# Five engines' written orders of one step, replaced by other orders of the same calls

## The reference

```
q, k, v = split(einsum(x, w_qkv) + b_qkv)        # q, k rotated
weights = softmax(mask(q k / sqrt(192) + alibi))
h = h + einsum(weights v, w_out) + b_out
```

## Time and profile before

| | |
|---|---|
| median of 3 runs | 1754.96 us (1750.04 to 1756.24) |
| the profiled execution | 1752.32 us, of which the span of the instructions is 1750.5 us |
| busy, of the span | TensorE 95%, VectorE 84%, ScalarE 76%, GpSimd 64% |
| mean granted TensorE clock | 0.976 of full |
| transfers | 113.70 MB, on average 65 GB/s |
| chain that ended last | 88% TensorE, 4% VectorE, 3% SyncE's queue, 2% GpSimd |

### The profile page before, as it was taken

The page is one execution under the profiler, slowest core; times in us unless marked ns, Lnnn a source line. Parts: engine busy times, 40 slices in busy tenths (PEclk is TensorE's granted clock), DMA queues, the critical chain, the costliest instruction groups (busy, mean ns, idle before and its releaser), DMA issues.

```text
span 1750.5 us, 48653 instructions
## 1 busy us (share of the span) xinstructions
PE 1664.2 (95%) x16742; PEld 1278.3 (73%) x16742; DVE 1470.0 (84%) x4972; ACT 1323.6 (76%) x3812; POOL 1120.1 (64%) x1034
## 2 busy tenths in 40 slices
PE   7758999999999999999999999999999999999975
PEld 6635777777777777777777777777777777777653
DVE  3837888899888888899888888899888888889874
ACT  0326888888888888888888888888888888888762
POOL 0087667766777666766777667666677667666500
PEclk9789999999999999999999999999999999999986
DMA  9311111111111111111111111111111111111100
GB/s 320 110 61 61 56 53 56 53 67 57 61 68 68 59 61 57 50 65 62 56 68 68 66 55 60 54 56 66 55 64 68 68 53 61 56 53 62 44 7 13
DMA packets 90168, 113.70 MB, mean 65 GB/s; under 512 B 14818, under 2 KB 52163, under 8 KB 89667
## 3 DMA queue, kind: packets, MB, share of 16 engines
q1 hardware_dynamic: 89922, 110.59, 18.1%
HBM read 26.62 MB, written 8.42 MB: 20 GB/s over the span
## 4 chain that ended last, share of the span: by engine, by line
PE 88%; DVE 4%; SPq 3%; POOL 2%; ACT 1%; issue 1%; DMA 0%; DVEq 0%; POOLq 0%; ACTq 0%
PE bank L725 45%; PE bank L842 9%; PE bank L983 7%; PE bank L831 6%; PE bank L829 6%; PE bank L994 3%; PE bank L853 3%; PE bank L903 3%; PE bank L891 2%; PE bank L1003 2%; SPq L320 1%; PE bank L882 1%; DVE arena L1283 1%; PE bank L950 0%; POOL rot L486 0%
## 5 line engine op out<-in xcount | busy, mean ns | idle before, releaser
L482 POOL TENSOR_TENSOR arena<-rq,cos 128x512 f32<-128x512 f32 x256 | 326.1, 1274 | 280.0 <-ACT rq L526 280.0
L535 ACT ACTIVATE arena<-arena,nm 128x129 f32<-128x129 f32 (+1 forms) x1024 | 455.6, 455 | 0.0
L486 POOL TENSOR_TENSOR rot<-rot,sin 128x512 f32<-128x512 f32 x256 | 326.3, 1275 | 103.9 <-DMA rot<-rq 103.9
L725 PE MATMUL bank<-xt_h,weights 128*128 128x256 f16 x2048 | 378.9, 273 | 9.2 <-ACT rq L526 7.8
L526 ACT ACTIVATE rq<-bank,bqk 128x256 f32<-128x256 f32 x512 | 214.4, 471 | 170.1 <-PE bank L725 155.3
L1283 DVE CUSTOM_DVE_ANT_0 arena<-bank,bias 128x129 f32<-128x129 f32 (+1 forms) x1024 | 317.9, 352 | 26.5 <-issue 16.6
L489 POOL TENSOR_TENSOR arena<-arena,rot 128x512 f32<-128x512 f32 x256 | 314.2, 1228 | 37.3 <-POOL rot L486 0.9
L1291 DVE TENSOR_TENSOR ptr_l<-bank,ptr_h 128x384 f16<-128x384 f32 x512 | 280.0, 552 | 31.8 <-ACT ptr_h L545 29.4
L545 ACT ACTIVATE ptr_h<-bank 128x384 f16<-128x384 f32 x512 | 249.1, 486 | 68.6 <-PE bank L725 44.0
L725 PE MATMUL bank<-xt_l,weights 128*128 128x256 f16 x1024 | 279.6, 273 | 0.0
L842 PE MATMUL bank<-eye,arena 128*128 128x128 f32 x1536 | 253.0, 277 | 8.5 <-DVE ptr_l L1291 4.4
(11 more groups left out here) (200 smaller groups left out, 3182.5 us busy)
## 6 DMA issues: line engine op xcount, KB each, us to landing
rot<-rq SPq DMA_DIRECT2D x512, 128.0 KB, 2.0
arena<-in_x SPq DMA_DIRECT2D x4, 2048.0 KB, 15.2
xin<-in_x SPq DMA_DIRECT2D x32, 256.0 KB, 2.8
hr<-hr SPq DMA_DIRECT2D x32, 256.0 KB, 2.3
out<-h SPq DMA_DIRECT2D x64, 128.0 KB, 2.1
arena<-in_L_attn_w_qkv SPq DMA_DIRECT2D x2, 1536.0 KB, 8.6
weights<-in_L_ffn_w_down SPq DMA_DIRECT2D x1, 1024.0 KB, 11.8
arena<-in_L_ffn_w_gate SPq DMA_DIRECT2D x1, 1024.0 KB, 8.5
```

Of the source, the lines that this page charges most:

```text
L482: pool.tensor_tensor(dst, rq[:, g % 2].rearrange("p j (t n) -> p j t n", t=T), cos[:, :].rearrange("p (t n) -> p t n", t=T).unsqueeze(1).b ...
L486: pool.tensor_tensor(r, r, sin[:, :].unsqueeze(1).broadcast_to([P, 2, SIDE]), ALU.mult).then_inc(t2_ready, 1)
L535: act.activation(cols, cols, ACT.Exp, bias=nm[:, t, h:h + 1], scale=-1.0, accum_out=rs[:, t, h:h + 1]).then_inc(e_done, 1)
L725: ins = pe.matmul(dst, lhs[l], rhs[r], start=start and n == 0, stop=stop and n == len(parts) - 1)
```

## The change

The calls of each step are the same in number and in what they issue. Their order changes, and with it the image index of each relative to s (a call moved over the end of the list comes with another index, which alone changes nothing). SyncE and GpSimd, whole:

```diff
             def step(s):
+                rotate(s - 1, 0)
+                rotate(s - 1, 1)
+                rotate(s - 1, 2)
+                store(s - 3, 0)
+                move(s - 2)
                 rotate(s - 1, 3)
                 rotate(s - 1, 4)
+                rotate(s - 1, 5)
                 load(s + 1)
-                rotate(s - 1, 5)
                 rotate(s - 1, 6)
                 rotate(s - 1, 7)
                 store(s - 3, 1)
-                rotate(s, 0)
-                rotate(s, 1)
-                rotate(s, 2)
-                move(s)
-                store(s - 2, 0)
```

```diff
             def step(s):
+                rotate(s, 5)
+                row_operators(s + 2)
+                rotate(s, 6)
+                add_bias(s + 1)
+                rotate(s, 7)
                 rotate(s + 1, 0)
                 rotate(s + 1, 1)
                 rotate(s + 1, 2)
-                row_operators(s + 2)
                 token_rstd(s)
                 rotate(s + 1, 3)
                 rotate(s + 1, 4)
-                rotate(s + 1, 5)
                 image_rstd(s + 2)
-                rotate(s + 1, 6)
-                rotate(s + 1, 7)
-                add_bias(s + 2)
```

TensorE's list goes from the first to the second; here the parts that the text below speaks of:

```diff
-                scores(s - 1, 7)
-                values(s - 1, 9)
-                transposes(s - 1, 11)
-                project_v(s, 2)
-                turn_inner(s - 1, 0)
-                transposes(s - 1, 12)
-                values(s - 1, 10)
-                transposes(s - 1, 13)
-                values(s - 1, 11)
-                project_v(s, 3)
-                scores(s, 0)
-                gate_up(s - 1, 3)
-                turn_input(s + 1)
-                values(s - 1, 12)
-                transposes(s - 1, 14)
-                out_transposes(s - 1, 2)
...
-                turn_inner(s - 1, 1)
-                transposes(s, 2)
-                values(s - 1, 15)
...
+                project_v(s + 1, 2)
+                transposes(s, 12)
+                values(s, 10)
+                scores(s, 7)
+                values(s, 11)
+                project_v(s + 1, 3)
+                transposes(s, 13)
+                turn_inner(s, 0)
+                transposes(s, 14)
+                scores(s + 1, 0)
+                values(s, 12)
+                values(s, 13)
+                out_transposes(s, 2)
+                turn_input(s + 2)
+                gate_up(s, 3)
+                transposes(s, 15)
...
+                values(s, 15)
...
+                turn_inner(s, 1)
+                transposes(s + 1, 2)
+                values(s + 1, 0)
+                scores(s + 1, 3)
+                down(s, 1)
+                out_transposes(s, 3)
+                transposes(s + 1, 3)
```

VectorE's list, the beginning and what goes from its middle:

```diff
-                evict_scores(s - 3, 15)
-                normalise_image(s - 1)
-                normalise(s - 3, 2)
...
-                residual(s - 2)
-                weights_lo(s - 2, 4)
-                token_scales(s - 2)
-                normalise(s - 2, 0)
-                weights_lo(s - 2, 5)
+                weights_lo(s - 2, 4)
+                evict_scores(s - 2, 9)
+                normalise(s - 2, 0)
+                image_out(s)
+                reciprocals(s - 2, 1)
+                weights_lo(s - 2, 5)
+                image_stats(s)
+                weights_lo(s - 2, 6)
+                attended_lo(s - 2, 0)
+                gate(s - 2, 0)
+                evict_scores(s - 2, 10)
+                normalise_image(s)
+                gate_up(s - 2, 0)
+                weights_lo(s - 2, 7)
+                inner_peak(s - 2, 0)
+                weights_lo(s - 2, 8)
+                gate(s - 2, 1)
+                evict_scores(s - 2, 11)
...
+                residual(s - 1)
+                token_scales(s - 1)
+                evict_scores(s - 1, 8)
```

More of the change, by code:

```diff
@@ L1020, in step @@
             def step(s):
[L1021 to L1038, removed]
-                transposes(s - 1, 6)
-                turn_tokens(s - 1)
-                values(s - 1, 4)
-                values(s - 1, 5)
-                out_transposes(s - 1, 0)
-                project(s, 5)
-                scores(s - 1, 5)
-                gate_up(s - 1, 0)
-                transposes(s - 1, 7)
-                project(s, 6)
@@ L1049, in step @@
-                transposes(s - 1, 8)
-                gate_up(s - 1, 1)
-                values(s - 1, 6)
-                project(s, 7)
-                transposes(s - 1, 9)
-                values(s - 1, 7)
-                scores(s - 1, 6)
-                project_v(s, 0)
-                transposes(s - 1, 10)
-                values(s - 1, 8)
-                gate_up(s - 1, 2)
-                out_transposes(s - 1, 1)
-                project_v(s, 1)
-                scores(s - 1, 7)
-                values(s - 1, 9)
@@ L1078, in step @@
[L1078 to L1091 removed]
+                values(s, 3)
@@ new lines, in step @@
+                project(s + 1, 3)
+                transposes(s, 4)
+                scores(s, 4)
+                project(s + 1, 4)
+                coarse(s + 2)
+                transposes(s, 5)
+                synthesise(s + 2)
+                transposes(s, 6)
+                scores(s, 5)
+                turn_tokens(s)
+                values(s, 4)
+                project(s + 1, 5)
+                out_transposes(s, 0)
+                gate_up(s, 0)
+                project(s + 1, 6)
+                transposes(s, 7)
@@ new lines, in step @@
+                transposes(s, 8)
+                values(s, 5)
+                values(s, 6)
+                project(s + 1, 7)
+                gate_up(s, 1)
+                values(s, 7)
+                project_v(s + 1, 0)
+                transposes(s, 9)
+                transposes(s, 10)
+                scores(s, 6)
+                values(s, 8)
+                project_v(s + 1, 1)
+                out_transposes(s, 1)
+                gate_up(s, 2)
+                transposes(s, 11)
+                values(s, 9)
@@ new lines, in step @@
+                transposes(s, 15)
+                values(s, 14)
+                scores(s + 1, 1)
+                project(s + 2, 0)
+                transposes(s + 1, 0)
+                down(s, 0)
+                values(s, 15)
+                project(s + 2, 1)
+                transposes(s + 1, 1)
+                scores(s + 1, 2)
+                project(s + 2, 2)
+                turn_inner(s, 1)
+                transposes(s + 1, 2)
+                values(s + 1, 0)
+                scores(s + 1, 3)
```

189 lines of the change are left out of this document (85 added, 104 removed).

## The result

The changed kernel took **1765.07 us** (median of 6, 1759.75 to 1767.73), the kernel before, run beside it, 1754.1 us (6 runs, 1750.04 to 1756.24). The ratio is 1.0066, with a 95% interval of 1.0052 to 1.0080: slower by 0.66%, just over the 0.5% of the prediction and 2 us above its range. The profiled execution took 1764.7 us with a span of 1762.9, against 1752.3 and 1750.5: 12.4 us of span to find.

The account below looks back on a forecast made before the run. TensorE, busy throughout the middle, was taken as the bound; -8 - 3 + 3 + 1 = -7 us on the profiled 1752.3 gave 1745.3, and with 2.6 us to the median 1748 us, range 1738 to 1763.

Parts of the forecast that it names:

- What bounds the kernel: Middle: TensorE is busy throughout, so a new order can win at the ends and lose on some 30 steps.
- 1, the filling: Beginning: earlier row_operators on GpSimd shortens the stalls before coarse(1) and coarse(2); -8 us, bounds -12 and -3.
- the rival: Beginning: both stalls gone, slow clock avoided, nothing late in the middle; -16 us, 1739 us, chance 0.10.
- 2, TensorE's order: Middle: three transposes a step no longer follow values, 0.1 us a step; -3 us, bounds -3 and 0.
- 3, the waits in the middle: Middle: shorter distances give small stalls, normalise_image's delay is covered; 0.1 us a step, +3 us, bounds 0 and +15.
- The sign that I named for this: Middle: steps of 49.4 us or more, TensorE loads waiting for VectorE's L1283 or L1291, L1428 at 2.2 us.
- The rival was the truth: Middle: normalise_image collides fully with GpSimd, 0.5 us a step at scores(6); +15 us, 1760 us, chance 0.18.
- the other terms: Beginning, TensorE's order in the middle, and end: -8, -3 and +1 us.
- 4, SyncE: SyncE's queue: move(c) goes behind the next image's rotations and load(a) one rotation back; nothing gained or lost.
- 5, the end: Last image's attention: shorter scores(7) to transposes(14) is exposed without projections to cover it; +1 us, bounds -2 and +4.

Follow-up runs that it names:

- experiment 4: Changed kernel, calls in place, normalise_image's two TENSOR_SCALAR in an accumulator form that leaves out the scaling by rstd; 1743.84 us, ratio 0.9943 to the kernel before.
- experiment 10: Changed kernel with normalisation on ScalarE, its shift kept in unused columns of gs instead of a new tile; 1740.79 us, ratio 0.9930 to the kernel before.
- The control: Kernel before, order untouched, with normalise_image in the accumulator form that leaves out the scaling by rstd; 1751.40 us, ratio 0.9992.
- experiment 8: Changed kernel with normalise_image in the accumulator form, plus row_operators back behind the third rotation in GpSimd's list; 1761.37 us, ratio 1.0050 to the kernel before.

## Why the prediction was wrong

**What bounds the kernel: right.** TensorE bounds the middle, a new order can lose there on every step, and it did.

**1, the filling (-8, bounds -12 and -3): right in kind, 2 us too much.** It gave -5.9. coarse(1) started at 104.82 (I said near 104), project_v(0, 0) at 118.25 (118.9), coarse(2) at 148.21 with no idle piece. What I said would be late next, image 0's residual chain, was: transposes(6) waits for it. The kernel after:

```profile
148.21 1.46 PE L903 MATMUL bank<-s,rowop 128*128 128x256 f32 x6
...
153.10 0.55 PE L842 MATMUL bank<-eye,arena 128*128 128x128 f32 x3 [2.24 <-DVE ptr_l L1291]
```

so that project(1, 5) starts at 155.01 and not at 153.5. Another 0.75 us went to the collision in the filling (experiment 4), which brings the order's own filling to -6.7; the remaining 0.65 that experiment 4 is ahead is its preparation. That coarse(2) would run at the full clock (1.46 us for 2.93) I had only in the rival.

**2, TensorE's order (-3): the size came right, by luck.** With the collision gone the thirty steps take 1468.1 us (experiment 4) for 1471.1, and 1465.8 in experiment 10. The control alone took 1469.5, so 1.4 to 5.3 us is what can be said. The reason that I gave did not do it. In the 29 steps of either kernel that have the same sequence of calls, the distances from start to next start add up for transposes to 5.51 us a step in the kernel before and to 5.75 in experiment 4. No transposes call costs 0.36 behind values any more, as I had counted, but five for one now stand ahead of scores, as here in experiment 4:

```profile
818.17 0.49 PE L842 MATMUL bank<-eye,arena 128*128 128x128 f32 x3
818.59 0.49 PE L829 MATMUL bank<-arena 64*128 64x129 f32 x4
```

That distance is 0.42 us where it is 0.33 ahead of most others; I had looked only at what stands in front of a transposes call. What fell is project_v (5.38 to 5.19 us a step), coarse and synthesise (2.35 to 2.16) and project (10.60 to 10.52), together more than the transposes lost: 49.05 to 48.86.

**3, the waits in the middle (+3, bounds 0 and +15): the step that failed.** It measured +20.3 (1488.4 - 1468.1). Nothing came of the short distances that I had walked (transposes(14), scores(0), values(15)): experiment 4 has them all and loses nothing by them. The collision did all of it, and the sentence that failed is "GpSimd has just ended cos and waits for its DMA there by my walk, so I take a third, all covered". GpSimd began L482 at 804.03, had 0.7 us of it left when the pair began at 804.60, and went straight on to L486 at 805.27; in 21 of 29 steps both its instructions caught one of the pair. In the other 8 it did wait for its DMA, as my walk had it, and the second of the pair went free. Whether 1.4 us is paid hung on less than a microsecond between the two engines, which my walk did not have. The cover was mis-sized as well. I counted the slack of evict_scores(11) ahead of scores(6) and a wait for tanh, 1.0 us together, and overlooked the nearer user: VectorE's gate_up stands right behind the pair, and TensorE's next gate_up waits for it. The steps above show a cover of 0.4 us at most. By my cover of 1.0 us the same delays would have left about 10 us over the 29 steps (16 x 0.39 + 5 x 0.84, an estimate from the groups above), so the phase and the cover failed about equally. The sign that I named for this came in part: steps of 49.4 us or more, the pair at 2.0 us in the mean, but TensorE waited for VectorE's L1445 and not for L1283 or L1291.

**The rival was the truth and priced too low.** It had the place, the mechanism and the sign, but 0.5 us a step and 1760 where it was 0.68 and 1765, and I gave it 0.18. By its own sum it only undoes the other terms (10 us) from 0.33 us a step, and reaches 0.5% from about 0.6; so its price of 0.5 and 1760 did not make the kernel slower by 0.5%, though most of its chance was counted there. The argument against it, that TensorE runs on in the kernel before with VectorE just as full, was none: there the pair ran beside an idle GpSimd. The rule that I cited from the Trainium skill, taken in full, named the right case, and the earlier trace rows had shown it four times out of four; a third of it was a choice with no row behind it.

**4, SyncE: right**: the one wait for a load that is new, GpSimd's for xin in the filling, is 0.5 us. **5, the end (+1): right**, +1.0, all of it ahead of the last attention_out (45.6 us for 44.5), in the last image's own attention.

**The sum.** Without term 3 it is -10, 1742.3 on the profiled execution and 1745 as a median; the order without its collision measured 1743.84. That it fits so well is in part luck, with term 1 at -6.7 for -8 and term 2 for another reason.

## What to carry to other kernels

When a VectorE instruction like these (TENSOR_SCALAR, 128x256, from SBUF to SBUF) is moved, ask what GpSimd does at that moment before asking where there is room: here it lasted for the rest of GpSimd's instruction plus 0.15 us, and a pair of them was caught twice. Where the two engines' phases can't be told to within one GpSimd instruction, price the full collision and take the cover from the nearest user. The repair need not be a new place: another engine for the same arithmetic left the order as it was and gave 24 us, and another form, which leaves out the scaling, 21 us.

## What the runs showed of the hardware

- Even a TENSOR_SCALAR of 128x2 is caught: 1.26 us for 0.17; it ends 0.02 to 0.03 us behind GpSimd's instruction, where one of 128x256 ends 0.15 behind. A TENSOR_SCALAR of 128x1 is not caught: in the kernel after over 200 of them began inside a GpSimd instruction and none took over 0.28 us, as when alone. An accumulator's form of 128x256 costs 0.53 + 0.08 us for 0.41 and is never caught, in five kernels.
- A pair back to back is caught twice: GpSimd's next instruction starts before the second of the two, which made 2.00 to 2.63 us of 0.73.
- With a tile of 8 bytes more ahead of the tiles that are loaded, the first loads took 30.8 us for 25.7 in SyncE's queue, and the kernel 1745.26 for 1740.79. One kernel with the tile stands behind this.
- The filling of experiment 8 shows what a lower clock takes: between 110 and 130 us, at 0.70 of the full clock for 0.94 in the kernel before, the starts of three project calls were 3.7 us apart for 2.4, and attention_out(1) came 2.9 us later with the same two stalls.
- A transposes call (three matmuls of 128x128, f32) is followed by the next start after 0.33 us as a rule, and after 0.42 where that is scores (64x129, f32).
